# Two pair layers on one core: x of five chunks transposed in the first stage, u kept in q's PSUM bank, and both layers' orders written anew

## The reference

```python
# layer 0 (pair_repr = x; n = 1, s and r run over 128, channels 32)
x = layernorm(pair_repr, ln1_w, ln1_b)
left  = sigmoid(x @ left1)  * (x @ left2)
right = sigmoid(x @ right1) * (x @ right2)
p = einsum('nsre,nkre->nske', left, right)
p = layernorm(p, ln2_w, ln2_b)
g = sigmoid(x @ gate)
x1 = pair_repr + (p @ out_w) * g
# layer 1
left = x1 @ W_left + b_left + x1 @ W_eq + b_eq
right_sum = sum over axis 2 of (x1 @ W_right + b_right)
out = left * right_sum * sigmoid(x1 @ W_gate + b_gate)
out = layernorm(out @ W_out + b_out + x1, ln_scale, ln_bias)
```

## Time and profile before

| what | value |
|---|---|
| time, median of 3 runs (lowest to highest) | 103.02 us (102.84 to 103.04) |
| the profiled execution: time, span | 102.81 us, 100.9 us |
| mean granted clock of TensorE | 0.967 |
| PE busy | 85.2 us, 85% of the span |
| PEld busy | 65.3 us, 65% |
| DVE busy | 70.8 us, 70% |
| ACT busy | 70.1 us, 70% |
| POOL busy | 60.5 us, 60% |
| stores: KB each, median from issue to landing | 256, 3.3 us |

### The profile page before, as it was taken

How to read it: one execution, slowest core, us unless ns; L and a number is a source line. 1 busy time by engine, 2 the same in 40 slices (tenths; PEclk the granted TensorE clock), 3 DMA queues, 4 the chain that set the end, 5 groups by cost and what they waited for, 6 DMA issues and landing times. The chain is left out here.

```text
span 100.9 us, 1793 instructions
## 1 busy us (share of the span) xinstructions
PE 85.2 (85%) x546; PEld 65.3 (65%) x546; DVE 70.8 (70%) x283; ACT 70.1 (70%) x112; POOL 60.5 (60%) x76
## 2 busy tenths in 40 slices
PE   0978968998999999999999799998999999993000
PEld 0956855766787899553454677875887978853000
DVE  0587698936667500499994949965899989898670
ACT  0639979999876265697479944599199999967300
POOL 5158689969970100008642769549998898996300
PEclk9999999999999999999999999999999999999655
DMA  3999998000000000000000000000042015579476
GB/s 48 189 155 146 146 146 87 10 0 0 0 0 10 0 0 0 0 0 0 3 0 0 0 10 0 0 0 0 0 67 43 0 27 77 78 117 147 74 111 97
DMA packets 33544, 4.51 MB, mean 45 GB/s; under 512 B 33408, under 2 KB 33536, under 8 KB 33536
## 3 DMA queue, kind: packets, MB, share of 16 engines
q1 hardware_dynamic: 31776, 4.03, 32.6%
q10 hardware_dynamic: 1760, 0.38, 2.0%
HBM read 2.31 MB, written 2.10 MB: 44 GB/s over the span
## 5 line engine op out<-in xcount | busy, mean ns | idle before, releaser
L357 POOL TENSOR_TENSOR t_tok<-p_sb,rstd 128x512 f32<-128x512 f32 x7 | 10.1, 1451 | 13.2 <-DVE rstd L725 13.2
L916 PE MATMUL bank<-lr_blk,xnT 64*128 64x256 f32 x128 | 15.6, 387 | 1.7 <-ACT xnT L451 1.4
L653 DVE TENSOR_TENSOR lr<-bank,sig_lr 128x512 f32<-128x512 f32 x16 | 10.9, 688 | 6.0 <-ACT sig_lr L461 6.0
L916 PEld LDWEIGHTS bank<-lr_blk,xnT 64*128 64x128 f32 x128 | 11.9, 186 | 4.2 <-ACT xnT L451 1.9
L719 DVE BATCH_NORM_STATS2 stats<-p_sb 128x6 f32<-128x64 f32 x64 | 8.5, 208 | 7.3 <-ACT p_sb L503 7.3
L365 POOL TENSOR_TENSOR x_low<-x1T,x_high 128x512 fp32r<-128x512 f32 x6 | 7.7, 1292 | 5.2 <-ACT x_high L539 5.2
L461 ACT ACTIVATE sig_lr<-bank 128x512 f32<-128x512 f32 x16 | 9.3, 598 | 1.8 <-PE bank L916 1.6
L440 ACT ACT_TABLE_LOAD x8 | 10.3, 1283 | 0.1
L1106 PEld LDWEIGHTS bank<-wout_blk,oT 128*128 128x128 f32 x64 | 8.0, 191 | 3.6 <-POOL oT L373 2.5
L293 POOL TENSOR_TENSOR xc<-x_tok,stats 128x512 f32<-128x512 f32 (+1 forms) x8 | 8.0, 1010 | 3.7 <-DVE stats L638 3.6
L1106 PE MATMUL bank<-wout_blk,oT 128*128 128x128 f32 x64 | 8.7, 279 | 1.8 <-POOL oT L373 1.8
(11 more groups left out here) (102 smaller groups left out, 187.8 us busy)
## 6 DMA issues: line engine op xcount, KB each, us to landing
x_tok<-in_x SPq DMA_DIRECT2D x14, 128.0 KB, 4.2
out<-sq SPq DMA_DIRECT2D x7, 256.0 KB, 3.3
x_tok<-in_x SPq DMA_DIRECT2D x3, 64.0 KB, 3.0
w_rep<-in_weights ACTq DMA_DIRECT2D x4, 45.1 KB, 3.2
out<-sq ACTq DMA_DIRECT2D x1, 128.0 KB, 2.5
out<-sq SPq DMA_DIRECT2D x1, 128.0 KB, 2.5
x_tok<-in_x ACTq DMA_DIRECT2D x1, 64.0 KB, 2.7
row_rep<-in_rows SPq DMA_DIRECT2D x1, 32.0 KB, 4.0
```

Source lines behind the costliest of these rows:

```text
L357: nc.gpsimd.tensor_tensor(place(t_tok[:, c % 2], 0, SPC), even_first(p_sb[:, :, s]), even_first(rstd[:, 1:2, s]).to_broadcast([P, 2, SPC / ...
L653: nc.vector.tensor_tensor(lr[:, :, s, :].rearrange("p q s t -> p s q t"), src[:, :, 2 * CH:4 * CH].rearrange("p s (q t) -> p s q t", t=2), ...
L916: last = nc.tensor.matmul(dst, xnT[half, c, k * P:(k + 1) * P], lr_blk[half].rearrange("p g m c -> p g (m c)"), start=True, stop=True, ski ...
```

## The change

x of chunks 0 to 4 (HOIST = 5) is turned in the first stage, into banks that the left/right projections use at other times, and copied to SBUF, into the tensor sq that is otherwise written only in layer 1: chunks 0, 3 and 4 by ACT (below), 1 and 2 by DVE (a tensor_copy). x of chunk 4 is turned behind the last left/right projection. Chunks 5 to 7 are turned where they were. XT being free until then, q of chunks 0 to 4 alternates between the banks Q and XT, and u of these chunks is written over q in its bank; add_x reads x from SBUF and u from PSUM. The eight filling matmuls go. The orders of all engines are written anew in the first stage and in the layers behind it; two of POOL's scales go to DVE and two of DVE's biases to POOL, and the order of the stores follows.

```diff
+HOIST = 5
+EARLY_X = [6, 7, 6, 7, 5]
-POOL_SCALES = [0, 2, 3, 4, 5, 6]
-POOL_BIASES = [0, 2, 4]
-DVE_SCALES = [1]
-DVE_BIASES = [3, 1, 5, 6]
-STORES = [0, 2, 3, 4, 1, 5, 6]
+POOL_SCALES = [0, 2, 4, 5]
+POOL_BIASES = [0, 2, 4, 3, 6]
+DVE_SCALES = [1, 3, 6]
+DVE_BIASES = [1, 5]
+STORES = [0, 1, 2, 4, 5, 3, 6]
...
+        def x_feature(c):
+            return sq[:, c * SPC:(c + 1) * SPC, :].rearrange("p s c -> p (s c)")
+        def q_bank(c):
+            return XT if c < HOIST and c % 2 else Q
...
+            def copy_x(c):
+                act.wait_ge(xT_ps, c + 1)
+                nc.scalar.activation(x_feature(c), bank[:, EARLY_X[c]], ACT.Copy).then_inc(x_copied[c], 1)
...
             def residual0(c):
                 dve.wait_ge(q_ps, c + 1)
                 dve.wait_ge(g_ready, c + 1)
-                link(nc.vector.scalar_tensor_tensor(out=u[:, c % 2], in0=bank[:, Q], scalar=q_bias[:], in1=gT[:, c],
+                dst = bank[:, q_bank(c)] if c < HOIST else u[:, c % 2]
+                link(nc.vector.scalar_tensor_tensor(out=dst, in0=bank[:, q_bank(c)], scalar=q_bias[:], in1=gT[:, c],
                                                     op0=ALU.add, op1=ALU.mult))
             def add_x(c, first=0, last=BLK):
-                dve.wait_ge(xT_ps, c + 1)
+                if c < HOIST:
+                    dve.wait_ge(x_copied[c], 1)
+                else:
+                    dve.wait_ge(xT_ps, c + 1)
...
+                    in0 = x_feature(c)[:, b] if c < HOIST else bank[:, XT, b]
+                    in1 = bank[:, q_bank(c), b] if c < HOIST else u[:, c % 2, b]
...
+            def transpose_x(c):
+                if c < HOIST:
+                    for n in (2 * c, 2 * c + 1) if c == 0 else (c + 1,):
+                        pe.wait_ge(x_in[n], arrived(n))
+                    if c == 4:
+                        pe.wait_ge(lr_ready, 14)
+                    elif c >= 2:
+                        pe.wait_ge(x_copied[c - 2], 1)
+                    b = EARLY_X[c]
+                else:
+                    pe.wait_ge(x1_ready, BLK * c)
+                    b = XT
...
             def project_q(c):
                 pe.wait_ge(tT_ready, c + 1)
-                if c:
+                if c < 2:
+                    pe.wait_ge(p_ready, q_bank(c) + 1)
+                elif c <= HOIST:
+                    last = max(n for n in range(c) if q_bank(n) == q_bank(c))
+                    pe.wait_ge(x1_ready, BLK * (last + 1))
+                else:
                     pe.wait_ge(x1_ready, BLK * (c - 1) + 1)
...
             pool.wait_ge(consts, 1 + 2 * GRP)
+            pool.wait_ge(w_in, 16 * GRP)
+            left_right_block()
             centre(1)
+            centre(2)
             normalise1(1)
```

More of the change, by code:

```diff
@@ L182, in mat @@
             return w_rep[:, i:i + CH]
+        x_copied = [sem(f"x_copied{c}") for c in range(HOIST)]
         x_in = [sem(f"x_in{b}") for b in range(len(SUMS1))]
@@ L490, in _ @@
             sigmoid_lr(4, 0)
+            affine1(7)
             sigmoid_lr(4, 1)
-            affine1(7)
             sigmoid_lr(5, 0)
+            affine1(8)
             sigmoid_lr(5, 1)
[L495 to L498, removed]
+            sigmoid_lr(6, 0)
+            sigmoid_lr(6, 1)
+            sigmoid_lr(7, 0)
+            sigmoid_lr(7, 1)
+            copy_x(4)
             for b in range(8):
@@ L575, in _ @@
             gate0(6)
+            high1(1)
+            gate1(0)
             gate0(7)
@@ L681, in _ @@
             statistics1(5)
+            copy_x(2)
+            inverse1(4)
+            multiply_lr(0, 0)
+            statistics1(6)
             multiply_lr(0, 1)
-            inverse1(4)
-            statistics1(6)
+            statistics1(7)
             multiply_lr(1, 0)
-            statistics1(7)
+            statistics1(8)
             multiply_lr(1, 1)
-            statistics1(8)
+            inverse1(5)
             multiply_lr(2, 0)
-            inverse1(5)
             multiply_lr(2, 1)
-            for c in range(3, CHUNKS):
-                for h in range(2):
-                    multiply_lr(c, h)
+            multiply_lr(3, 0)
+            multiply_lr(3, 1)
+            multiply_lr(4, 0)
+            multiply_lr(4, 1)
+            multiply_lr(5, 0)
+            multiply_lr(5, 1)
+            multiply_lr(6, 0)
+            multiply_lr(6, 1)
+            multiply_lr(7, 0)
+            multiply_lr(7, 1)
             dve.wait_ge(bo_ps, 1)
@@ L925, in _ @@
             pe.wait_ge(centre_ready, 1)
-            def fill(b, times):
-                for _ in range(times):
-                    nc.tensor.matmul(bank[:, b, 0:P], ident[:], ident[:], start=True, stop=True)
+            def transpose_x(c):
[10 more added lines that the diff above has]
+                    b = XT
+                for j in range(BLK):
+                    s = c * SPC + j * GRP
+                    last = nc.tensor.transpose(bank[:, b, j * P:(j + 1) * P],
+                                               x_tok[:, s:s + GRP, :].rearrange("p s c -> p (s c)"), ident[:])
+                last.then_inc(xT_ps, 1)
             transpose_xn(0)
-            transpose_xn(1)
+            transpose_x(0)
+            transpose_x(1)
             pe.wait_ge(lr_blk_ready, 1)
             project_lr(0, 0)
+            transpose_xn(1)
+            transpose_x(2)
+            transpose_x(3)
+            transpose_xn(2)
             project_lr(0, 1)
-            fill(6, 4)
-            transpose_xn(2)
-            fill(6, 3)
+            transpose_xn(3)
+            pe.wait_ge(x_copied[2], 1)
+            pe.wait_ge(x_copied[3], 1)
             project_lr(1, 0)
+            transpose_xn(4)
             project_lr(1, 1)
-            transpose_xn(3)
-            transpose_xn(4)
             project_lr(2, 0)
+            transpose_xn(5)
             project_lr(2, 1)
             project_lr(3, 0)
-            pe.wait_ge(xnT_ready, 5)
-            fill(0, 1)
             project_lr(3, 1)
-            transpose_xn(5)
             transpose_xn(6)
@@ L991, in project_gate0 @@
                 nc.tensor.matmul(bank[:, b], gate0_blk[:], xnT[:, c], start=True, stop=True).then_inc(g_ps, 1)
-            def transpose_x(c):
-                if c:
-                    pe.wait_ge(x1_ready, BLK * c)
-                else:
-                    pe.wait_ge(p_ready, XT + 1)
-                for j in range(BLK):
-                    s = c * SPC + j * GRP
-                    last = nc.tensor.transpose(bank[:, XT, j * P:(j + 1) * P],
-                                               x_tok[:, s:s + GRP, :].rearrange("p s c -> p (s c)"), ident[:])
-                last.then_inc(xT_ps, 1)
             for c in range(4):
                 project_gate0(c)
-            transpose_x(0)
             project_gate0(4)
```

173 lines of the change are left out of this document (89 added, 84 removed).

## The result

The changed kernel takes **101.34 us** (median of 4 runs, 101.28 to 101.58), before took 102.97 beside it (102.84 to 103.04). The ratio is 0.9848, with a 95% interval of 0.9828 to 0.9867: faster by 1.63 us. The forecast was 101.0. The profiled execution took 101.28 us, 1.53 less than that of before. In what follows medians are over all runs of a kernel, while ratios leave disturbed runs out, so that a median can lie above what its ratio says.

The account below looks back on a forecast made before the run. It saw PE full in the left/right projections, no engine full from 54 to 71, DVE, POOL and PE nearly full from 71.0. Stores -2.1 and first stage +0.25 sum to -1.85: 102.81 becomes 101.0 us, range 100.1 to 102.9.

Parts of the forecast that it names:

- Entry: From x1 of chunk 1 (54.0) to u(5): DVE's waits fall from 5.1 to 2.0 us, u(5) 2.6 us earlier.
- The fourth wait: DVE's wait for q of chunk 5: 0.95 us for 1.49, since q(5) must wait until x1(4) is complete, about 67.3.
- First stage: Up to the P stage: PE's full stretch starts as before; x(4) behind the last projection costs +0.25 us.
- The copies: x copies on ACT and DVE ahead of the root, forecast 0; rival that they are not covered: up to 2.6, 103.55 us, chance 0.14.
- Fills: First stage: removing the filling passes on PE costs 0, since they filled waits.
- The clock rival: First stage: without filling passes PE's clock falls to 1.2 GHz, two half chunks add 1.2 us: 102.2 us, chance 0.12.
- u in PSUM: DVE writing u to a PSUM bank: 0 to 0.05 us either way per instruction, 0.5 at most; taken as 0.
- Dense block: From u(5) to o_a(7): stays 19.6 us long, so the entry's 2.6 us carry over.
- end of DVE: After o_a(7): POOL's bias ahead of its last product gives 0.5 back, less alternation saves 0.1; DVE ends at 95.7.
- The stores: Last transfer ends at 97.8 for 100.05, by five stores of 1.8 us or DVE's end alike; 2.1 us gained.
- The rival with POOL: DVE's scales on POOL, now at other places: three meet POOL where DVE waits, 1.5 us goes back: 102.5 us, chance 0.13.

Follow-up runs that it names:

- the run with x(4) late: Changed kernel with x of chunk 4 transposed in the third stage behind q(4), and u(4) in SBUF: 101.82 us, ratio 0.9873.
- The exchange of biases: Changed kernel with DVE adding the bias of chunk 3 and POOL that of chunk 5, chunk 3 stored before 5: 100.96 us, ratio 0.9795.
- the row in PSUM: Changed kernel with the bias row copied once into an unused part of a PSUM bank, where DVE's biases read it: 100.39 us, ratio 0.9752.

## Why the forecast came out

**Entry, -2.6 and +0.25 forecast, -2.51 measured.** The size holds, the account of it only in part. The prediction said that from 54 to 71 no engine is full, and named DVE, ACT and POOL. The earlier trace rows have PE there at 16.11 of 17.0 us: PE was the bound, and DVE's waits for gates and q were in the main its queue seen from DVE. The table above tells the two shares. The new orders take away PE's own stalls, 0.56 us for a gate and 0.28 for tT(5) in the trace of before: from q(1) to q(5) its chain is 1.4 shorter by them. The other 0.6 were not followed one by one; a part is longer hand-overs behind a stall, as 0.40 between the sums and y(0) for 0.14. The hoist takes 4 x 0.44 = 1.76 us of work off PE, of which 1.1 arrive. ACT's order by itself is worth 0.4, and without it the hoist and the other orders win next to nothing there: 18.77 for 18.86.

**The fourth wait.** The prediction put it down to x1(4), which q(5) must wait for. Without that condition q(5) still had to queue on PE. In the changed kernel x1(4) ends at 67.17, and PE is through with the gate's matmul at about 67.18 (its start and the 0.23 to the next one in the run with x(4) late); q(5) begins at 67.33, so x1(4) adds 0.15 at most. That q(5) began where the forecast had it, at 67.3, is in part luck: two conditions met, and the prediction knew one.

**First stage, +0.25 forecast, +0.18 measured, for another reason.** The way from the last root to the P stage is what it was (13.14 for 13.15), so the 0.18 lie in the root. Kernels with this same way to the root had it anywhere from 20.27 to 21.01, so one trace can't settle 0.2. x(4) costs 0.06 and not 0.23: the prediction counted the last bias product with its whole 0.36, while the P stage begins 0.23 behind that product's start (33.20 and 33.43). The copies were covered, as it said; a second set was not.

**Fills, 0 forecast.** True of this change as a whole, but not for the reason given, that they filled waits: with neither fills nor x transposes the clock fell, and the traces differ by 0.5 us. The clock rival was real and its place right; it did not come about since the x transposes kept the clock at 1.00. The Trainium skill (TensorE: Matmul & The Clock Gate, Part 4: PE-mode transpose) states that transposes do not count as busy time for the clock in the way of other matmuls. This case's traces do not agree: from 9.95 to 12.0 us the changed kernel's PE did transposes alone, and the clock stayed at 1.00 where it fell without those of x. Whether transposes can also raise it from 0.50 no run here shows.

**u in PSUM, 0 forecast.** u itself took 0.755 us for 0.731, so the term holds. The prediction priced the write and overlooked the read. With x in SBUF, u in SBUF as well would have cost 3.9 us; u in q's bank is what makes the hoist pay. The Trainium skill (SBUF — State Buffer, SBUF: two separate sides) has the rule: a VectorE instruction with two SBUF inputs and a GpSimd instruction that reads SBUF exclude each other for the whole length of the one that starts first. The traces agree: 1.20 and 1.47 for 0.34 beside POOL, and 1.51 against 0.69 with one input moved to PSUM. POOL's add behind it gives way too: 1.71 against 1.27.

**Dense block, 0 forecast, +0.3 measured; end of DVE, +0.4 forecast, 0 measured.** The loss sat elsewhere than said: POOL's last product kept its 1.03, while o_a(7) waited 1.09 us for PE. Against the forecast the two nearly cancel.

**The stores, -2.1 forecast, the last transfer some 2.2 behind a DVE end at 95.7.** DVE ended at 95.75, but the last transfer came 2.73 behind it. This is the mis-sized term, 0.6 of gain lost against before (2.15). The prediction had the right formula (the first of the last stores, and four or five of 1.8 us behind it), but took chunk 5 as ready at 89.4. It was ready at 90.23, since its bias stood still beside POOL's product. 90.23 + 1.0 + 4 x 1.8 = 98.4 is the end that the trace shows. The exchange of biases and the row in PSUM gave 0.4 and 0.95 back.

Together: -2.51 + 0.3 + 0 + 0.6 = -1.6, against -1.53 between the profiled executions. Against the forecast's own terms the entry came out 0.2 better, the dense block 0.3 worse, the end of DVE 0.4 better and the stores 0.5 worse. That only some 0.3 us is left of these is partly luck. The rival with POOL was this mechanism, at one place where DVE waited for it instead of three.

## What to carry to other kernels

Read every engine's busy time in a stretch before calling it free: a wait on one engine for many small results of another is often that other engine's full queue, and work taken off that queue pays only as far as nothing else in it stalls. When a tile moves from PSUM to SBUF, look at the second input of each VectorE instruction that reads it, and at what GpSimd does at that moment; one input in PSUM, even a 32-column row, keeps the two apart. At the end of a kernel work backwards from the store queue: here the chunk ahead of which it last ran dry set the end, not DVE's last instruction.

## What was not expected of the hardware

A VectorE instruction of 0.34 us took 1.47 us beside GpSimd, and ended 0.13 to 0.16 us behind the other's end in all seven cases of one trace. Dependent halves (scale, bias, scale, bias) of 256 columns took 1.67 us where the same four in independent pairs took 1.42. Kernels with one and the same first stage up to its last root had that root up to 0.7 us apart (20.27 to 21.01 in nine traces), while the way from it to the P stage was the same within 0.07. The cause of that scatter stays open. Sixteen transposes kept TensorE's granted clock at 1.00 where it otherwise fell to 0.50.
